# Softplus in a fused FFN–scan–FFN kernel: correction term kept in SBUF, z in two PSUM banks, one ScalarE table set

## The chip, the core and the metric

The kernel runs on one core of a Trainium2 chip. The metric is the device time of one execution in microseconds (us). The engines that matter here are TensorE (PE in the profile, its weight loads PEld), VectorE (DVE), ScalarE (ACT), GpSimd (POOL) and the queue of SyncE (SP), which issues most transfers. Each engine takes its instructions in the order in which they stand in its own program; semaphores tie the engines together.

## The reference

```python
x = x + 0.5 * ffn(layernorm(x), ...)          # x: (4, 512, 256) float32
x = x + attn(layernorm(x), W_x, W_dt, b_dt, A_log, D)
x = x + 0.5 * ffn(layernorm(x), ...)

def attn(x, W_x, W_dt, b_dt, A_log, D):       # a selective scan, 16 states per channel
    x_proj = x @ W_x.T
    dt_x, Bm, Cm = split(x_proj, [R, R + N], axis=-1)       # R = 64, N = 16
    dt = softplus(dt_x @ W_dt.T + b_dt)
    A = -exp(A_log)
    dA = exp(einsum('bld,dn->bldn', dt, A))
    dBx = einsum('bld,bln,bld->bldn', dt, Bm, x)
    h = dA_t * h + dBx_t ; y_t = einsum('bdn,bn->bd', h, C_t)   # for t in order
    return ys + x * D
```

The ffn is a shared expert (gate, up, down) and eight routed experts, of which each token takes one. The change touches only dt = softplus(...) of the middle step and what hangs on it.

## The kernel before, in words

The work has three stages: the first ffn, the scan, the second ffn. In the scan the 4 sequences (batches b) of 512 positions are done one after the other, and in each batch the 16 states n one after the other: state number s = 16 b + n runs from 0 to 63. Channels lie on the 128 partitions in KC = 2 halves k, positions along the free dimension, so a state is a tile of 128 x 1024.

For one state:
- ScalarE computes the decay, `da = exp(a_neg * dt)` (decay, L663, two instructions), three states ahead of the recurrence.
- The input term is `dtx_t * B` with positions on partitions. VectorE and ScalarE share it by quarters (outer, L1405 on VectorE, L679 on ScalarE; the table BY_DVE says how many quarters VectorE takes: 0 for most states), and TensorE transposes it into PSUM (turn_dbx, L1030). For six states of a batch (table DIAG) TensorE forms it itself as a product with a diagonal matrix (L1037), and there is no outer.
- VectorE runs the recurrence over 1024 elements, `hs` (L1421), reading `da` in SBUF and the input term in PSUM.
- GpSimd multiplies it by the row of C, `gs = hs * c_sb` (L523). Both inputs are in SBUF. It runs at most two states ahead of TensorE's add.
- TensorE adds the products, transposed, into the PSUM banks YA (add, L1054), in order; when the 16 states of a batch are added, VectorE adds YA to `x_sb` (add_y, L1457).

While batch b is scanned, the engines prepare dt, B and C of batch b + 1, with these steps put at fixed states n of the loops: project (L983, one matrix product with W_x) into bank T, project_copy on ScalarE (L630) to `proj`, project_bt (L994, TensorE transposes B into bank Y; L1361, VectorE copies it to `b_t`, a part of the tile `h_sb`), project_z (L1003, z = dt_x W_dt^T, one half k at a time, both halves through the one bank T), and then softplus. With w = exp(-|z + b|), softplus is max(z + b, 0) + log(1 + w), and a correction w - ((1 + w) - 1) puts back what the rounding of 1 + w loses. Before: ScalarE takes |z + b| (L636) and max(z + b, 0) (L637) out of the bank, w (L641), 1 + w back into the bank (L650, for b > 0) and the logarithm (L657); VectorE forms the correction in the bank (L1370; for batch 0 it forms 1 + w too, L1373 and L1375), adds the logarithm in the bank (L1381) and then the maximum (L1384), one half at a time. The exponential and the logarithm are in different table sets as loaded here, so each logarithm in the loop has a table load ahead of it (L657) and one behind it (L663). TensorE then transposes dt (turn_dt, L1014) and VectorE multiplies it with xn into `dtx_t` (L1390).

GpSimd also normalises rows for the next stages (L469, SBUF to SBUF): eight instructions ahead of batch 0, then four in each of the batches 0 to 2.

Of the kernel before, what the change touches and what calls it, by code (L numbers as in the profile page):

```python
# [27 lines left out]
def macaron_kernel(nc, x, w_xT, w_dtT, b_dt, a_log, d_skip, router_w, gate_w, up_w, down_w,  # L28
# [47 lines left out]
    with ExitStack() as ctx:  # L76
# [26 lines left out]
        neg_half = sb("neg_half", [P, LT])  # L103
        e_less = sb("e_less", [P, E])
# [123 lines left out]
        pj_all, pj_copy, pj_bt, pj_btc, pj_z, pj_abs, pj_max, pj_exp, pj_u, pj_w, pj_rest, pj_ln, pj_sum, pj_dt, pj_tp, pj_dtx = (  # L228
            sem(f"pj_{s}") for s in ("all", "copy", "bt", "btc", "z", "abs", "max", "exp", "u", "w", "rest", "ln", "sum", "dt", "tp",
# [191 lines left out]
        def _(pool):  # L421
# [135 lines left out]
        def _(act):  # L557
# [85 lines left out]
            def project_u(b, k):  # L643

                if k == 0:
                    act.wait_ge(pj_exp, b + 1)
                    act.wait_ge(pj_max, KC * (b + 1))
                else:
                    act.wait_ge(pj_dt, KC * b + 1)
                nc.scalar.activation(pj_bank(b, k), w_exp[:, k], ACT.Identity, bias=1.0).then_inc(pj_u, 1)  # L650

            def project_ln(b):

                act.wait_ge(pj_exp, b + 1)
                if b > 0:
                    act.wait_ge(pj_sum, KC * b)
# [894 lines left out]
```

## Time and profile before

| what | value |
|---|---|
| median of 3 runs | 441.34 us (440.18 to 441.75) |
| the profiled execution | 441.44 us, of which the span from first to last instruction is 439.6 us |
| busy shares of the span | PE 92%, VectorE 75%, GpSimd 64%, ScalarE 63% |
| mean granted TensorE clock | 0.996 of full speed |
| first ffn, until the scan's first recurrence | 0 to 142.8 us |
| scan, 64 states | 142.8 to about 333 us |
| second ffn | about 333 to 439.6 us |

The shares are means over three stages with different limits. In the scan VectorE, GpSimd, ScalarE and TensorE are all busy most of the time, so there the order in which one releases the other has to be read from the timeline.

### The profile page before, as it was taken

The page shows a single profiled execution, that of the slowest core. Times are in us where ns is not written, and L with a number is a line of the kernel's source. Part 1 is how long each engine was busy: PE and PEld are TensorE (multiplying, and loading weights), DVE is VectorE, ACT ScalarE, POOL GpSimd, SP SyncE. Part 2 cuts the span into 40 slices and gives each one's busy share as a digit, 9 for nine tenths or more (in the row PEclk, how much of TensorE's full clock was granted, in tenths as well). Part 3 has the DMA queues.
Part 4 walks back from the last instruction along what each step waited for, and adds up shares of the span by engine and source line. Part 5 has one row for each costly group of instructions (what it writes and reads, how often), then busy time and mean ns, then how long its engine had stood idle before and what let it go on. Part 6 is the DMA issues. An engine that isn't in the chain of part 4 may idle for free. (4 is left out here: it accounts for less than half of the span.)

```text
span 439.6 us, 8329 instructions
## 1 busy us (share of the span) xinstructions
PE 402.4 (92%) x2716; PEld 278.4 (63%) x2716; DVE 329.5 (75%) x518; ACT 275.0 (63%) x501; POOL 281.1 (64%) x216
## 2 busy tenths in 40 slices
PE   6899899999996899899989997989999899899995
PEld 5537444444454689777977797879994556344452
DVE  4678565553388988999999999989887775456552
ACT  1430465564248799897999899997962210556553
POOL 7204356643328589997999799988891006487553
PEclk9899999999999999999999999999999999999999
DMA  8958115842604226463536453443320534334311
GB/s 250 385 179 264 48 54 167 284 174 101 204 10 91 73 82 180 81 144 106 186 75 118 141 176 73 115 157 92 121 72 0 172 107 120 99 118 135 111 60 48
DMA packets 50808, 56.84 MB, mean 129 GB/s; under 512 B 16329, under 2 KB 35597, under 8 KB 50768
## 3 DMA queue, kind: packets, MB, share of 16 engines
q1 hardware_dynamic: 46624, 45.78, 35.0%
q0 software_dynamic: 4144, 10.54, 8.0%
q8 instruction: 23, 0.38, 0.4%
q14 instruction: 17, 0.14, 0.1%
HBM read 41.14 MB, written 16.48 MB: 131 GB/s over the span
## 5 line engine op out<-in xcount | busy, mean ns | idle before, releaser
L523 POOL TENSOR_TENSOR gs<-hs,c_sb 128x1024 f32<-128x1024 f32 x63 | 148.3, 2380 | 18.7 <-DVE hs L1421 11.4
L1421 DVE TENSOR_TENSOR_SCAN hs<-da,bank 128x1024 f32<-128x1024 f32 x64 | 144.1, 2273 | 4.1 <-PE bank L1030 2.1
L663 ACT ACTIVATE da<-dt_sb,a_neg 128x511 f32<-128x511 f32 x128 | 84.5, 713 | 2.4 <-DVE dt_sb L1384 1.2
L1054 PE MATMUL bank<-ident,gs 128*128 128x128 f32 x504 | 66.3, 275 | 7.5 <-POOL gs L523 5.9
L1054 PEld LDWEIGHTS bank<-ident,gs 128*128 128x128 f32 x504 | 55.9, 141 | 12.1 <-POOL gs L523 9.8
L679 ACT ACTIVATE dbx_t<-dtx_t,h_sb 128x256 f32<-128x256 f32 x145 | 62.1, 498 | 1.6 <-DVE dtx_t L1390 1.4
L879 PE MATMUL bank<-xnT,w_gu 128*128 128x512 f32 x112 | 50.8, 601 | 0.0
L1030 PE MATMUL bank<-ident,dbx_t 128*128 128x128 f32 x336 | 44.2, 274 | 6.8 <-DVE hs L1421 4.1
L477 POOL DMA_INDIRECT da<-rows,row_token x29 | 30.6, 1055 | 29.7 <-DVE row_token L1292 21.2
L1030 PEld LDWEIGHTS bank<-ident,dbx_t 128*128 128x128 f32 x336 | 37.5, 141 | 12.2 <-DVE hs L1421 5.9
L591 ACT ACTIVATE th<-bank,da 128x256 f32<-128x256 f32 x36 | 17.0, 473 | 43.1 <-PE bank L918 30.4
L918 PE MATMUL bank<-w_gu,tt 128*128 x72 | 35.6, 616 | 3.2 <-ACT tt L596 2.2
L498 POOL DMA_INDIRECT token_out<-y_sb,row_token x18 | 19.0, 1056 | 29.2 <-DVE y_sb L1338 26.3
L477 POOL DMA_INDIRECT da<-rows,row_half x14 | 14.7, 1054 | 35.5 <-DVE row_token L1297 27.2
L1328 DVE TENSOR_TENSOR h_sb<-th,bank 128x256 f32<-128x256 f32 x36 | 15.1, 420 | 28.0 <-ACT th L591 27.9
L915 PE MATMUL bank<-w_gu,tt 128*32 x72 | 34.3, 598 | 1.4 <-ACT tt L596 1.4
L879 PEld LDWEIGHTS bank<-xnT,w_gu 128*128 128x128 f32 x112 | 21.0, 194 | 22.4 <-issue 22.3
L915 PE MATMUL bank<-dtx_t,tt 128*32 128x512 f32 x72 | 34.3, 598 | 0.0
L574 ACT ACTIVATE hs<-bank 128x512 f32<-128x512 f32 x10 | 6.0, 597 | 40.0 <-PE bank L879 34.6
L596 ACT ACTIVATE tt<-bank 128x512 f32<-128x512 f32 (+1 forms) x40 | 22.1, 553 | 13.6 <-PE bank L933 12.3
L498 POOL DMA_INDIRECT out<-y_sb,row_token x18 | 19.8, 1098 | 16.1 <-DVE y_sb L1341 8.2
L562 ACT ACTIVATE xnT<-bank 128x512 f32<-128x512 f32 x24 | 13.9, 590 | 17.3 <-PE bank L807 17.2
(184 smaller groups left out, 787.1 us busy)
## 6 DMA issues: line engine op xcount, KB each, us to landing
c_sb<-c_dram SPq DMA_DIRECT2D x64, 256.0 KB, 3.3
rows<-xn_no SPq DMA_DIRECT2D x8, 516.0 KB, 5.4
diag_dram<-dbx_t SPq DMA_DIRECT2D x6, 512.0 KB
routing<-diag_dram SPq DMA_DIRECT2D x11, 256.0 KB, 2.8
slot_m<-diag_dram SPq DMA_DIRECT2D x11, 256.0 KB, 2.9
rows<-xn_no SPq DMA_DIRECT2D x1, 2064.0 KB, 9.4
x_sb<-in_x SPq DMA_DIRECT2D x4, 512.0 KB, 6.4
w_gu<-in_gate_w SPq DMA_DIRECT2D x2, 1024.0 KB, 10.2
```

Of the source, the lines that this page charges most:

```text
L477: nc.gpsimd.indirect_dma_start(out=xr[:, u, lo:hi], out_offset=None, in_=source, in_offset=bass.IndirectOffsetOnAxis(ap=row, axis=0), boun ...
L498: nc.gpsimd.indirect_dma_start(out=rows_back, out_offset=bass.IndirectOffsetOnAxis(ap=row_token[:, TILE[j]:TILE[j] + 1], axis=0), in_=y_sb ...
L523: nc.gpsimd.tensor_tensor(gs[:, s % 2], hs[:, s % RING], c_sb[:, s % RING].unsqueeze(1).to_broadcast([P, KC, L]), ALU.mult).then_inc(sc_g, 1)
L596: nc.scalar.activation(tt[:, (j + 1) % 2, lo:hi], T[:, lo * P:hi * P].rearrange("p (a t) -> p a t", t=P), ACT.Copy).then_inc(ff_tpc, 1)
L663: nc.scalar.activation(da[:, s % RING, k, 1:L], dt_sb[:, k, seq(s // N)][:, 1:L], ACT.Exp, scale=a_neg[:, k, s % N:s % N + 1]).then_inc(sc ...
L679: step = nc.scalar.activation(plain_buffer(s)[:, i, :], dtx_t[:, b % 2, i, :], ACT.Copy, scale=b_t[:, b, i, n:n + 1])
L879: last = nc.tensor.matmul(shared_banks(r, b, fo)[h], w_gu[:, k, SHARED, h * F + fo * P:h * F + (fo + 1) * P], xnT[:, k, b * L:(b + 1) * L] ...
L915: last = nc.tensor.matmul(H[j % 2][part, :], tt[:, j % 2, 2 + k, part], gu_part(i, g)[:, k, :] if g else w, start=(k == 0), stop=(k == KC ...
L918: last = nc.tensor.matmul(H[j % 2][:, :], tt[:, j % 2, 2 + k], w, start=(k == 0), stop=(k == KC - 1))
L1030: mm = nc.tensor.transpose(DBX[s % 2][:, k, i * P:(i + 1) * P], plain_buffer(s)[:, i, k * P:(k + 1) * P], ident[:])
L1054: mm = nc.tensor.matmul(YA[k][:, i * P:(i + 1) * P], products[:, k, i * P:(i + 1) * P], ident[:], start=(s % N == 0 and i == 0), stop=(s % ...
L1421: nc.vector.tensor_tensor_scan(hs[:, s % RING].rearrange(flat), da[:, s % RING].rearrange(flat), DBX[s % 2][:, :, :].rearrange(flat), 0.0, ...
```

## The change

- For batches 1 to 3 z is kept in two banks, T for k = 0 and Y for k = 1 (`pj_bank`). Bank Y held the transposed B, from which VectorE's outer read; outer now reads the copy `b_t` in SBUF.
- B is transposed and copied earlier, since z needs bank Y: on TensorE project_bt stands ahead of turn_dbx at n = 2, 1, 0 of the batches 0, 1, 2 (before: at n = 3), on VectorE the copy stands at n = 3, 2, 1 (before: 4).
- ScalarE no longer takes max(z + b, 0). It writes -(1 + w) once for both halves, 128 x 1024, into an SBUF tile (`neg_u`: half of `dtx_t` for batch 0, `y_sb` later).
- VectorE forms the correction there, (-(1 + w) + 1) + w, in one instruction of 1024 with both inputs in SBUF (project_rest), then max(z + b, correction) per half with z in PSUM (project_max), then adds the logarithm in one instruction of 1024 with both inputs in SBUF (project_dt). dtx is one instruction of 1024 for b > 0.
- One table set that holds exponential and logarithm is loaded ahead of batch 0 and again after the hyperbolic tangent of the shared expert. In the last batch the hyperbolic tangent of the second ffn's first piece has a table load of its own (before: none there).

```diff
         def pj_bank(b, k):
-            return YA[k] if b == 0 else T
+            return (YA if b == 0 else (T, Y))[k]
+
+        def neg_u(b):
+            return dtx_t[:, 1].rearrange("p (k a) d -> p k (a d)", k=KC) if b == 0 else sg_h
...
             def project_abs(b, k):
                 act.wait_ge(pj_z, KC * b + k + 1)
                 if b > 0:
-                    act.wait_ge(pj_rest, KC * b)
+                    act.wait_ge(pj_rest, b)
                 nc.scalar.activation(w_exp[:, k], pj_bank(b, k), ACT.Abs, bias=b_sb[:, k:k + 1]).then_inc(pj_abs, 1)
-                nc.scalar.activation(dt_sb[:, k, seq(b)], pj_bank(b, k), ACT.Relu, bias=b_sb[:, k:k + 1]).then_inc(pj_max, 1)
...
-            def project_u(b, k):
-                if k == 0:
-                    act.wait_ge(pj_exp, b + 1)
-                    act.wait_ge(pj_max, KC * (b + 1))
-                else:
-                    act.wait_ge(pj_dt, KC * b + 1)
-                nc.scalar.activation(pj_bank(b, k), w_exp[:, k], ACT.Identity, bias=1.0).then_inc(pj_u, 1)
+            def project_u(b):
+                act.wait_ge(pj_exp, b + 1)
...
+                nc.scalar.activation(neg_u(b), w_exp[:], ACT.Identity, bias=neg_one[:, 0:1], scale=-1.0).then_inc(pj_u, 1)
...
             def project_bt(b):
                 pe.wait_ge(pj_copy, b + 1)
...
-                    pe.wait_ge(sc_dve, states_by("dve", N * (b - 1) + 4 + 3))
+                    pe.wait_ge(pj_btc, b)
...
             def project_z(b, k):
                 pe.wait_ge(pj_copy, b + 1)
                 if b > 0 and k > 0:
-                    pe.wait_ge(pj_max, KC * b + k)
+                    pe.wait_ge(pj_btc, b + 1)
...
-                    if more and n == 3:
+                    late = (2, 1, 0, 0)[b]
+                    if more and n == late:
                         project_bt(b + 1)
                     if s + 2 < STATES:
                         turn_dbx(s + 2)
...
-                nc.vector.tensor_tensor(pj_bank(b, k), log_w[:, k], pj_bank(b, k),
-                                        ALU.add if b == 0 else ALU.subtract).then_inc(pj_sum, 1)
-                dve.wait_ge(pj_sum, KC * b + k + 1)
-                nc.vector.tensor_tensor(dt_sb[:, k, seq(b)], pj_bank(b, k), dt_sb[:, k, seq(b)], ALU.add).then_inc(pj_dt, 1)
+            def project_rest(b):
+                dve.wait_ge(pj_u, b + 1)
+                nc.vector.scalar_tensor_tensor(out=neg_u(b), in0=neg_u(b), scalar=1.0, in1=w_exp[:],
+                                               op0=ALU.add, op1=ALU.add).then_inc(pj_rest, 1)
+
+            def project_max(b):
+                dve.wait_ge(pj_rest, b + 1)
+                for k in range(KC):
+                    nc.vector.scalar_tensor_tensor(out=neg_u(b)[:, k], in0=pj_bank(b, k), scalar=b_sb[:, k:k + 1], in1=neg_u(b)[:, k],
+                                                   op0=ALU.add, op1=ALU.max).then_inc(pj_max, 1)
+
+            def project_dt(b):
+                dve.wait_ge(pj_ln, b + 1)
+                dve.wait_ge(pj_max, KC * (b + 1))
+                nc.vector.tensor_tensor(dt_sb[:, :, seq(b)], log_w, neg_u(b), ALU.add).then_inc(pj_dt, 1)
...
                 nc.vector.tensor_tensor(plain_buffer(s)[:, LT - mine:, :], dtx_t[:, b % 2, LT - mine:, :],
-                                        B_T[:, b, LT - mine:, n:n + 1].to_broadcast([P, mine, D]), ALU.mult).then_inc(sc_dve, 1)
+                                        b_t[:, b, LT - mine:, n:n + 1].to_broadcast([P, mine, D]), ALU.mult).then_inc(sc_dve, 1)
```

Three places show how instructions move. In these lists the lines of the changed kernel differ by some 5 to 10 from those of the kernel before, the recurrence (L1421, now L1425) is named SCALAR_TENSOR_TENSOR, and x2 means two alike in a row.

TensorE at the seam from batch 1 to batch 2, before: the product with W_x (L983), the transposes of the input term (L1030) and the adds (L1054).

```order
L983 MATMUL bank<-xnT,w_x 96x512 x2
L1030 MATMUL bank<-ident,dbx_t 128x128 x8
L1054 MATMUL bank<-ident,gs 128x128 x8
L1003 MATMUL bank<-th,w_dt 128x512
L1030 MATMUL bank<-ident,dbx_t 128x128 x8
```

The same place in the changed kernel:

```order
L990 MATMUL bank<-xnT,w_x 96x512 x2
L1001 MATMUL bank<-ident,th 128x16 x4
L1035 MATMUL bank<-ident,dbx_t 128x128 x8
L1059 MATMUL bank<-ident,gs 128x128 x8
L1010 MATMUL bank<-th,w_dt 128x512
L1035 MATMUL bank<-ident,dbx_t 128x128 x8
```

The four transposes of B out of `proj` (the tile `th`) now stand right behind the product with W_x, ahead of the last add of batch 1. The same move is made in batch 0, where they stand ahead of turn_dbx(4).

VectorE in the middle of batch 1 (the recurrences of states 21 to 24 and what stands between), before:

```order
L1421 SCALAR_TENSOR_TENSOR hs<-da,bank 128x1024
L1370 SCALAR_TENSOR_TENSOR bank<-bank,w_exp 128x512
L1421 SCALAR_TENSOR_TENSOR hs<-da,bank 128x1024
L1381 TENSOR_TENSOR bank<-tt,bank 128x512
L1384 TENSOR_TENSOR dt_sb<-bank,dt_sb 128x512
L1421 SCALAR_TENSOR_TENSOR hs<-da,bank 128x1024
L1370 SCALAR_TENSOR_TENSOR bank<-bank,w_exp 128x512
L1405 TENSOR_TENSOR dbx_t<-dtx_t,bank 128x256
L1421 SCALAR_TENSOR_TENSOR hs<-da,bank 128x1024
```

In the changed kernel, from the recurrences of states 19 to 21 on:

```order
L1425 SCALAR_TENSOR_TENSOR hs<-da,bank 128x1024 x3
L1371 SCALAR_TENSOR_TENSOR y_sb<-y_sb,w_exp 128x1024
L1425 SCALAR_TENSOR_TENSOR hs<-da,bank 128x1024
L1378 SCALAR_TENSOR_TENSOR y_sb<-bank,b_sb,y_sb 128x512 x2
L1425 SCALAR_TENSOR_TENSOR hs<-da,bank 128x1024
L1385 TENSOR_TENSOR dt_sb<-tt,y_sb 128x2x512
L1409 TENSOR_TENSOR dbx_t<-dtx_t,h_sb 128x256
L1425 SCALAR_TENSOR_TENSOR hs<-da,bank 128x1024 x2
```

Every one of the steps before had one input in a PSUM bank; now L1371, L1385 and L1409 take both from SBUF tiles.

VectorE ahead of the first recurrence, before, from the correction to the first outer:

```order
L1373 TENSOR_SCALAR bank<-w_exp 128x512
L1375 TENSOR_TENSOR bank<-w_exp,bank 128x512
L1373 TENSOR_SCALAR bank<-w_exp 128x512
L1375 TENSOR_TENSOR bank<-w_exp,bank 128x512
L1381 TENSOR_TENSOR bank<-tt,bank 128x512
L1384 TENSOR_TENSOR dt_sb<-bank,dt_sb 128x512
L1381 TENSOR_TENSOR bank<-tt,bank 128x512
L1384 TENSOR_TENSOR dt_sb<-bank,dt_sb 128x512
L1390 TENSOR_TENSOR dtx_t<-bank,xn_no 128x512 x2
L1405 TENSOR_TENSOR dbx_t<-dtx_t,bank 128x512
```

The same stretch in the changed kernel:

```order
L1371 SCALAR_TENSOR_TENSOR dtx_t<-dtx_t,w_exp 128x1024
L1378 SCALAR_TENSOR_TENSOR dtx_t<-bank,b_sb,dtx_t 128x512 x2
L1385 TENSOR_TENSOR dt_sb<-tt,dtx_t 128x2x512
L1393 TENSOR_TENSOR dtx_t<-bank,xn_no 128x512 x2
L1409 TENSOR_TENSOR dbx_t<-dtx_t,h_sb 128x512
```

Eight instructions of 512 have become two of 512 and two of 1024.

## Rows read from the trace of the kernel before

**Rows 1.** Busy us by engine (PE, PEld, DVE, ACT, POOL), batch by batch

```profile
156.00:197.60 41.60, 38.85 (x315) 34.58 (x315) 38.62 (x37) 39.02 (x71) 40.67 (x21) 1.00 0.51 126
197.60:244.20 46.60, 43.99 (x353) 38.64 (x352) 45.11 (x42) 44.00 (x82) 43.81 (x23) 1.00 0.49 127
244.20:291.00 46.80, 43.27 (x353) 39.22 (x354) 45.52 (x41) 44.06 (x82) 43.93 (x23) 1.00 0.42 126
291.00:333.50 42.50, 40.66 (x321) 37.44 (x320) 38.58 (x34) 31.02 (x65) 34.06 (x18) 1.00 0.32 94
```

**Rows 2.** Timeline, GpSimd in batch 1: start, us, idle before in brackets

```profile
205.02 2.36 POOL L523 TENSOR_TENSOR gs<-hs,c_sb 128x1024 f32<-128x1024 f32 x1 [1.51 <-DVE hs L1421]
...
225.29 18.72 POOL L523 TENSOR_TENSOR gs<-hs,c_sb 128x1024 f32<-128x1024 f32 x8
```

**Rows 3.** Groups by line: busy us, mean ns, idle before and releaser

```profile
L523 POOL TENSOR_TENSOR gs<-hs,c_sb 128x1024 f32<-128x1024 f32 x63 | 148.3, 2380 | 18.7 <-DVE hs L1421 11.4 <-PE bank L1054 7.1
L1421 DVE TENSOR_TENSOR_SCAN hs<-da,bank 128x1024 f32<-128x1024 f32 x64 | 144.1, 2273 | 4.1 <-PE bank L1030 2.1 <-PE bank L1037 2.0
...
L637 ACT ACTIVATE dt_sb<-bank,b_sb 128x512 f32<-128x512 f32 x8 | 5.5, 682 | 0.0
...
L657 ACT ACT_TABLE_LOAD x4 | 5.1, 1283 | 0.1
...
L1357 DVE TENSOR_TENSOR x_sb<-xn_no,x_sb 128x1024 f32<-128x1024 f32 x3 | 3.7, 1222 | 2.7 <-DMA xn_no<-token_out 2.7
...
L1405 DVE TENSOR_TENSOR dbx_t<-dtx_t,bank 128x256 f32<-128x256 f32 x17 | 6.8, 402 | 0.1
...
L1381 DVE TENSOR_TENSOR bank<-tt,bank 128x512 f32<-128x512 f32 x8 | 5.5, 682 | 1.0 <-ACT tt L657 1.0
L1390 DVE TENSOR_TENSOR dtx_t<-bank,xn_no 128x512 f32<-128x512 f32 x8 | 5.3, 671 | 0.8 <-PE bank L1014 0.8
...
L1370 DVE SCALAR_TENSOR_TENSOR bank<-bank,w_exp 128x512 f32<-128x512 f32 x6 | 4.1, 678 | 0.7 <-ACT bank L650 0.7
```

**Rows 4.** Line L1450 (min/median/max ns), and the timeline around it

```profile
L1450 DVE TENSOR_TENSOR dbx_t<-hs,c_sb x2: 678/968/1259, 329.4 to 330.6; 128x512 f32<-128x512 f32 x2
...
327.78 2.35 POOL L523 TENSOR_TENSOR gs<-hs,c_sb 128x1024 f32<-128x1024 f32 x1 [0.52 <-PE bank L1054]
...
329.42 1.86 DVE L1450 TENSOR_TENSOR dbx_t<-hs,c_sb 128x512 f32<-128x512 f32 x2
```

**Rows 5.** Timeline ahead of the first recurrence, GpSimd and VectorE

```profile
131.37 9.65 POOL L469 TENSOR_SCALAR xn_no<-x_sb,mv,rstd 128x256 f32<-128x256 f32 x8
...
132.12 0.69 DVE L1373 TENSOR_SCALAR bank<-w_exp 128x512 f32<-128x512 f32 x1 [1.37 <-ACT w_exp L641]
...
136.83 0.69 DVE L1384 TENSOR_TENSOR dt_sb<-bank,dt_sb 128x512 f32<-128x512 f32 x1
...
142.78 2.28 DVE L1421 TENSOR_TENSOR_SCAN hs<-da,bank 128x1024 f32<-128x1024 f32 x1
```

**Rows 6.** Timeline of the first states of batch 0

```profile
145.15 4.87 POOL L523 TENSOR_TENSOR gs<-hs,c_sb 128x1024 f32<-128x1024 f32 x2 [4.12 <-DVE hs L1421]
...
148.07 0.41 DVE L1405 TENSOR_TENSOR dbx_t<-dtx_t,bank 128x256 f32<-128x256 f32 x1
...
153.96 1.04 PE L1030 MATMUL bank<-ident,dbx_t 128*128 128x128 f32 x8
...
154.16 0.59 ACT L630 ACTIVATE th<-bank 96x512 f32<-96x512 f32 x1 [2.26 <-PE bank L983]
```

**Rows 7.** Timeline at the seam from batch 1 to batch 2

```profile
240.52 1.88 PE L983 MATMUL bank<-xnT,w_x 128*96 128x512 f32 x4
...
242.68 0.58 ACT L630 ACTIVATE th<-bank 96x512 f32<-96x512 f32 x1
...
243.11 1.04 PE L1054 MATMUL bank<-ident,gs 128*128 128x128 f32 x8
...
244.19 1.28 DVE L1457 TENSOR_TENSOR x_sb<-x_sb,bank 128x512 f32<-128x512 f32 x2 [0.83 <-PE bank L1054]
```

More of the change, by code:

```diff
@@ L103, in macaron_kernel @@
         neg_half = sb("neg_half", [P, LT])
+        neg_one = sb("neg_one", [P, 1])
         e_less = sb("e_less", [P, E])
@@ L227, in macaron_kernel @@
         a_ready = sem("a_ready")
-        pj_all, pj_copy, pj_bt, pj_btc, pj_z, pj_abs, pj_max, pj_exp, pj_u, pj_w, pj_rest, pj_ln, pj_sum, pj_dt, pj_tp, pj_dtx = (
-            sem(f"pj_{s}") for s in ("all", "copy", "bt", "btc", "z", "abs", "max", "exp", "u", "w", "rest", "ln", "sum", "dt", "tp",
+        pj_all, pj_copy, pj_bt, pj_btc, pj_z, pj_abs, pj_max, pj_exp, pj_u, pj_rest, pj_ln, pj_dt, pj_tp, pj_dtx = (
+            sem(f"pj_{s}") for s in ("all", "copy", "bt", "btc", "z", "abs", "max", "exp", "u", "rest", "ln", "dt", "tp",
                                      "dtx"))
@@ L701, in scan @@
                         project_exp(1)
-                        project_u(1, 0)
-                    if b < BATCH - 1 and n == 7 + int(b == 0):
-                        project_u(b + 1, 1)
+                    if b == 0 and n == 5:
+                        project_u(1)
                     if b == 0 and n == 6:
@@ L1005, in turn_dt @@
             def turn_dt(b, h):
-                pe.wait_ge(pj_dt, KC * (b + 1))
-                if b > 0 and h > 0:
-                    pe.wait_ge(pj_dtx, 2 * b + h)
-                dst = YA[h] if b == 0 else T
+                pe.wait_ge(pj_dt, b + 1)
+                dst = pj_bank(b, h)
                 for i in range(2):
@@ L1089, in scan @@
                         skip(b, n - 5)
-                    if more and n - int(b == 0) in (8, 10):
-                        turn_dt(b + 1, (n - 8) // 2)
+                    if more and n - int(b == 0) in (8, 9):
+                        turn_dt(b + 1, n - int(b == 0) - 8)
                     turn = 12 if more else 9
@@ new lines, in project_dtx @@
+            def project_dtx(b):
+                halves = ((0, 1), (1, 2)) if b == 0 else ((0, 2),)
+                for lo, hi in halves:
+                    dve.wait_ge(pj_tp, 2 * b + hi)
+                    src = pair[3 if b == 0 else 1][:, lo:hi].rearrange("p h (i d) -> p (h i) d", d=D)
+                    nc.vector.tensor_tensor(dtx_t[:, b % 2, 2 * lo:2 * hi], src, xn[:, LT * b + 2 * lo:LT * b + 2 * hi, :],
+                                            ALU.mult).then_inc(pj_dtx, hi - lo)
@@ L1434, in scan @@
                         stats_of(2, b - 1)
-                    if more and n == 4:
+                    late = int(b == 0)
+                    if more and n == (3, 2, 1)[b]:
                         project_bt(b + 1)
-                    late = int(b == 0)
-                    if more and n in (5 + late, 7 + late):
-                        project_w(b + 1, (n - 5) // 2)
-                    if more and n in (6 + late, 8 + late):
-                        project_dt(b + 1, (n - 6) // 2)
-                    if more and n in (10 + late, 12 + late):
-                        project_dtx(b + 1, (n - 10) // 2)
+                    if more and n == 5 + late:
+                        project_rest(b + 1)
+                    if more and n == 6 + late:
+                        project_max(b + 1)
+                    if more and n == 7 + late:
+                        project_dt(b + 1)
+                    if more and n == 11 + late:
+                        project_dtx(b + 1)
             def last_product():
@@ L1492, in _ @@
             shared_hidden(0, 3, 0)
-            for k in range(KC):
-                project_w(0, k)
-            for k in range(KC):
-                project_dt(0, k)
-            for h in range(2):
-                project_dtx(0, h)
+            project_rest(0)
+            project_max(0)
+            project_dt(0)
+            project_dtx(0)
             outer(0)
```

42 lines of the change are left out of this document (15 added, 27 removed).

## The prediction

> **What bounds the kernel now.** I read the busy time of each engine batch by batch first. In a batch of the scan VectorE works 45 of 46.6 us, TensorE 44, ScalarE 44, GpSimd 44 [rows 1], so a share alone names no bound; the waits must. The timeline of GpSimd shows them: in batch 1, once its product of state 19 has started at 205.02, it runs without a gap through its other steps to the eight products that end at 244.0 [rows 2]; in batches 0 and 2 it does the same from the sixth and fifth state on. A product takes 2.38 us, a recurrence on VectorE 2.27 [rows 3] (2.2 from start to start), so VectorE makes its states a little faster and spends the rest on softplus and outer. For most of each batch GpSimd paces the adds and VectorE has little to spare. At a seam the order is fixed: TensorE's last add, then VectorE's add_y, which waited 0.83 us for it [rows 7], then the next recurrences. The ffn stages ahead of and behind the scan hold nothing of the change.
>
> **What the change takes away.** Per batch ScalarE loses two maxima of 0.68 us and, for batches 1 to 3, two table loads of 1.28 [rows 3], some 3.9 us. Nothing on the path waits for ScalarE but VectorE for 1.0 us before L1381 and 0.7 before L1370 in the whole run [rows 3]. VectorE loses eight steps of 0.67 to 0.69 [rows 3], 5.4 us, and gets three of 1024 at 1.22 (L1357 is the nearest row: two SBUF inputs, 1024) and two of 512 at 0.68, 5.0 us: 0.4 less. In a stretch that GpSimd paces, both savings hide behind GpSimd's products; where VectorE paced instead they would be worth 0.4 x 3 + 1.7 = 2.9 us.
>
> **What it adds: two SBUF inputs beside GpSimd.** No VectorE instruction of the scan before reads two SBUF tiles, but one: L1450. It ran twice, 512 wide, alike in shape: 1.26 us and 0.68 [rows 4]. The first was issued at 329.42, while GpSimd's product ran from 327.78 to 330.13, and ended at 330.68: it did next to nothing until GpSimd had finished and then needed 0.55 us. I take it that the two cannot read together. The page SBUF — State Buffer of the Trainium skill, section "Who interferes with whom", says the same: a VectorE instruction with two SBUF inputs contends with a GpSimd instruction that reads SBUF, the first to start holds the shared pair for its whole length and the other is fully blocked. By that rule the trace agrees (1.26 against 0.68), and it speaks against this change; with the rule the sum is the one below, and read the other way, as no collision, it is the first rival's.
>
> The change gives VectorE such steps in the middle of GpSimd's busy stretches: project_rest and project_dt once per batch, and every outer. If VectorE comes while GpSimd works, it waits for that product's end (0 to 2.38 us); then GpSimd's next one waits until VectorE is done. That second half no row shows. Bounds for what it costs GpSimd: nothing, to VectorE's whole step. I take what was left of the step in rows 4, 0.55 per 512: 1.1 us for 1024, 0.27 for an outer of 256. The steps, in order:
> - Ahead of the first recurrence. Without collisions this gets shorter: one maximum less ahead of w (about 0.57 from start to start), -(1 + w) at about 1.06 more, then 1.22, 1.2 and 1.22 in place of the steps from 132.12 to 137.52 [rows 5]: dt about 1.2 us earlier. But GpSimd normalises from 131.37 to 141.02, eight times 1.21 [rows 5]. Stepped: project_rest, ready at 132.6, has just missed the end at 132.58, runs from 133.8 to 134.9; the maxima to 136.2; project_dt at the next end, 137.3 to 138.4; the first outer to 141.3; the second waits for the last normalisation, pushed to 143.8; first recurrence at 144.95 against 142.78 [rows 5], +2.2. If project_rest slips in ahead of the instruction at 132.58, it comes at 143.85, +1.1. I take 1.7.
> - First states. The outer at 148.07 meets GpSimd's second product, which ends at 150.02 [rows 6]: +1.9 for the recurrence behind it, and for the add, project and all that follow. Then project_bt stands ahead of turn_dbx(4) and needs project_copy, which ended at 154.75 (154.16 + 0.59), where TensorE had started turn_dbx(4) at 153.96 [rows 6]: 0.8 of waiting and about 0.42 of transposes, 1.25. GpSimd had 0.4 us idle soon after, which swallows that much: 1.9 + 1.25 - 0.4 = 2.75.
> - The rest of batch 0, paced by GpSimd: project_rest and project_dt 2.2, outers of the states 10, 12, 16 and 17 at 0.27, 1.1: 3.3.
> - Batch 1: 2.2 and five outers (26, 28, 30, 32, 33), 1.35: 3.55. At its end TensorE's four transposes of B stand ahead of turn_dbx and the last add. They need project_copy, and that needs project, which ran from 240.52 to 242.4; the copy came at 242.68 to 243.26 on a ScalarE that was just free [rows 7]; now it may start 0.1 earlier. TensorE would stand from 242.24 to 243.2 and then transpose for 0.42: the add at 243.11 [rows 7] comes 1.4 later, and VectorE's add_y, already waiting for it, too. Of that 0.2 may be won back, as the add before starts the sooner: 1.2. Together 4.75.
> - Batch 2: 2.2 and three outers (42, 44, 46), 0.8: 3.0. Its seam has no such transposes.
> - Batch 3 has no outer on VectorE. Its one new table load, 1.28 [rows 3], stands on ScalarE with 31.0 of 42.5 us busy [rows 1] and three states ahead: 0.1.
> Sum: 1.7 + 2.75 + 3.3 + 4.75 + 3.0 + 0.1 = 15.6. The profiled execution took 441.44 us, its span 439.6 and 1.84 around it; the median is 441.34. **I predict 457.0 us.** Low end for the mechanism: half of the steps meet GpSimd between two products, about 449. High end: VectorE's waits, on average half a product, are not hidden but pace the batch. Six in batch 0, seven in 1, five in 2, each 1.2, less what VectorE had to spare (3.0, 1.5 and 1.3 us of idle time [rows 1], and the 0.4 saved): 3.8 + 6.5 + 4.3 in place of 3.3 + 3.55 + 3.0, about 462, and 466 with a start at +3.4 and a wait more at a seam.
>
> **Rivals.**
> *No collision worth speaking of.* The 1.26 us of L1450 had another cause (it is one instruction), or a step of 0.4 us finds a gap. Then: start -1.2, first states 1.25 - 0.4, the seam 1.2, the rest hidden by GpSimd's pace: +0.9, 442.3 us. Against it: the end of L1450 falls 0.55 us behind GpSimd's, as waiting would have it.
> *Faster.* No collision, and VectorE, not GpSimd, paces: then its 2.9 us come off and the start's 1.2, and the two stalls of TensorE are swallowed: 437.3 us. For it: VectorE has the highest busy time in batches 1 and 2 [rows 1]. Against it: GpSimd has no gap in the states 19 to 32 [rows 2], and add_y waits for an add that stands behind its product. It decides if VectorE's new steps of 1024 take 1.2 us in the scan and GpSimd's chain has gaps.
> *GpSimd does not let go.* Its instructions follow each other without a gap, so a waiting VectorE step could be passed over until GpSimd runs out of states. One product more, 2.38 less the 1.2 already counted, at each of the some 16 steps: +19, 476 us.
> *The table sets are not merged after all.* The order of the changed kernel has no table load around the logarithms; and ScalarE bounds nothing, so the time would not tell.
>
> **How the numbers follow.** Collision as stepped: 0.70, its own range 449 to 466. No collision: 0.15 (440.5 to 444.5). Faster: 0.08. GpSimd does not let go: 0.07. About 0.5%, 2.2 us, is what a measurement of this kernel can tell from no change. Slower by more: 0.70 + 0.07 + 0.03 of the no-collision case = 0.80; within: 0.11; faster: 0.08 + 0.01 = 0.09. The range reaches from 440.5, which takes in nearly all of the no-collision case, to 468, and leaves out the faster case, the last rival and a little more: 2 in 10.
>
> **What the profile of the changed kernel would show.** Right: L1409 (outer, 256) mean near 1 to 1.5 us in place of 0.40, with some at 0.40 and some over 2; L1371 and L1385 over 1.22, in the loop up to 3; gaps in GpSimd's chain of products right behind them; TensorE idle ahead of L1001 twice, near 0.8 and 1.0 us; the first recurrence at 144 to 145 us and a scan of about 204 us in place of 190; ScalarE some 12 us less busy and waiting. Wrong: L1409 at 0.40 throughout and GpSimd's chain without new gaps (no collision); the same with the first recurrence near 141.6 and shorter batches (faster); a GpSimd chain as before with VectorE steps of 3 to 5 us (the last rival). The sum would also be wrong if VectorE and GpSimd fall into step so that outers always come at a product's end: then only the 2.2 us per batch and the stalls of TensorE are left, near 450.

## The result, and the profile after

The changed kernel takes **456.66 us** (median of 4 runs, 455.58 to 458.0), the kernel before 440.81 beside it (440.18 to 441.75): ratio 1.036, 95% interval 1.032 to 1.040. It is slower by 3.6%, as predicted (457.0). The profiled execution took 456.64 us, its span 454.9, so 15.3 us more of span where the sum said 15.6. Of the four executions of e5 below, the longest, 459.67 us, was in the chip's slower state and is left out of its median and ratio.

The busy time of each engine from the first recurrence on, cut at VectorE's four add_y (columns: stretch, its length, PE, PEld, DVE, ACT, POOL, granted clock, DMA share, GB/s; compare [rows 1]), changed kernel:

```profile
142.58:204.51 61.93, 52.56 (x388) 45.50 (x387) 57.88 (x43) 45.35 (x85) 50.28 (x25) 0.97 0.42 103
204.51:255.03 50.52, 45.20 (x357) 39.09 (x356) 47.06 (x38) 40.86 (x77) 46.73 (x23) 1.00 0.44 115
255.03:302.75 47.72, 42.32 (x341) 37.75 (x342) 45.96 (x35) 38.52 (x73) 44.71 (x22) 1.00 0.40 114
302.75:347.45 44.70, 42.62 (x325) 39.83 (x324) 39.12 (x34) 33.87 (x69) 35.67 (x19) 0.96 0.30 95
```

Every batch is longer, the last too, and in the first and the last the mean clock is below 1. The same cuts in all kernels of this study (us, from the timeline of VectorE in each one's profiled execution; a fall is a stretch in which TensorE's granted clock is 0.50, 1.2 of 2.4 GHz, lasting 3.4 us where nothing else is said):

| kernel | first recurrence at | batch 0 | 1 | 2 | 3 | falls of the clock in it |
|---|---|---|---|---|---|---|
| before | 142.78 | 54.79 | 46.62 | 45.20 | 42.80 | none |
| after | 142.58 | 61.93 | 50.52 | 47.72 | 44.70 | batches 0, 3 |
| e1, before with outers from SBUF | 142.54 | 63.86 | 48.59 | 46.88 | 42.81 | batch 0: 6.8 us and 3.4 |
| e2, after, outers to ScalarE | 143.10 | 56.93 | 52.13 | 47.24 | 43.05 | batch 1 |
| e3, after, B's transposes late | 142.76 | 61.07 | 49.24 | 47.70 | 44.73 | batches 0, 3 |
| e5, after, operands in PSUM | 141.76 | 62.71 | 53.75 | 45.81 | 43.05 | batch 0: 6.8 us and 3.4; batch 1: 6.8 us |
| e10, e2 and e3 | 142.10 | 56.47 | 48.41 | 47.29 | 44.71 | batch 3 |
| e6, e2, e3 and e5 | 144.93 | 54.70 | 46.48 | 45.63 | 43.03 | ahead of the scan: two |
| e8, after, TensorE kept busy twice | 144.35 | 62.14 | 50.47 | 47.75 | 43.52 | ahead of the scan, batch 0 |
| e9, the same, three times | 143.25 | 61.04 | 50.50 | 47.75 | 43.52 | none |

What lies behind the last add_y is 107.4 us in both kernels. Groups by line, changed kernel (busy us, mean ns; outer, project_rest, project_dt of the loop, and GpSimd's normalisations):

```profile
L1409 DVE TENSOR_TENSOR dbx_t<-dtx_t,h_sb 128x256 f32<-128x256 f32 x17 | 13.1, 773 | 0.0
...
L1371 DVE SCALAR_TENSOR_TENSOR y_sb<-y_sb,w_exp 128x1024 f32<-128x1024 f32 x3 | 7.7, 2573 | 0.0
...
L1385 DVE TENSOR_TENSOR dt_sb<-tt,y_sb 128x1024 f32<-128x1024 f32 x3 | 5.0, 1651 | 0.0
...
L476 POOL TENSOR_SCALAR xn_no<-x_sb,mv,rstd 128x256 f32<-128x256 f32 x20 | 29.9, 1500 | 0.0
...
L1371 DVE SCALAR_TENSOR_TENSOR dtx_t<-dtx_t,w_exp 128x1024 f32<-128x1024 f32 x1 | 1.3, 1260 | 1.8 <-ACT dtx_t L658 1.8
```

Outer has a mean of 0.77 us where it had 0.40 [rows 3], and project_rest takes 2.57 in the loop where the one ahead of the loop, which came just as an instruction of GpSimd ended, took 1.26. GpSimd's normalisation, 1.21 each in [rows 5], has a mean of 1.50: it waits too. The timeline of batch 1 shows both directions:

```profile
215.82 5.67 POOL L530 TENSOR_TENSOR gs<-hs,c_sb 128x1024 f32<-128x1024 f32 x2
216.36 2.92 DVE L1371 SCALAR_TENSOR_TENSOR y_sb<-y_sb,w_exp 128x1024 f32<-128x1024 f32 x1
...
224.90 1.22 DVE L1385 TENSOR_TENSOR dt_sb<-tt,y_sb 128x1024 f32<-128x1024 f32 x1
225.02 2.44 POOL L476 TENSOR_SCALAR xn_no<-x_sb,mv,rstd 128x256 f32<-128x256 f32 x1
```

Project_rest is issued 0.54 us into a product, waits for its end and holds up the next: two products take 5.67 us in place of 4.76 (2 x 2.38, [rows 3]). Project_dt comes at 224.90, with 0.13 us left of the product that runs, takes its 1.22 us, and the normalisation behind it takes 2.44 (an outer follows project_dt at once).

The first states of batch 0, changed kernel (compare [rows 6]):

```profile
144.94 4.86 POOL L530 TENSOR_TENSOR gs<-hs,c_sb 128x1024 f32<-128x1024 f32 x2 [2.15 <-DVE hs L1425]
...
147.87 2.21 DVE L1409 TENSOR_TENSOR dbx_t<-dtx_t,h_sb 128x256 f32<-128x256 f32 x1
150.01 2.27 DVE L1425 TENSOR_TENSOR_SCAN hs<-da,bank 128x1024 f32<-128x1024 f32 x1
...
152.92 1.09 PE L1059 MATMUL bank<-ident,gs 128*128 128x128 f32 x8 [3.68 <-DVE x_sb L1308]
...
156.41 0.42 PE L1001 MATMUL bank<-ident,th 16*128 16x16 f32 x4 [0.68 <-ACT th L637]
```

The outer of state 4 took 2.21 us instead of 0.41 because GpSimd's second product had just begun. VectorE's next steps slip, TensorE's first add waits 3.68 us for one of them, and behind project it stands 0.68 us for project_copy. The granted clock in two stretches of 2 us of batch 0 (the column behind the five engines), and the transposes on TensorE at which the falls of batches 0 and 3 began, changed kernel:

```profile
194.00:196.00 2.00, 0.81 (x5) 0.81 (x6) 2.00 (x3) 0.83 (x2) 1.93 (x2) 0.87 0.86 88
196.00:198.00 2.00, 2.00 (x12) 2.00 (x10) 2.00 (x2) 2.00 (x5) 1.68 (x1) 0.50 0.59 165
...
195.19 1.73 PE L1035 MATMUL bank<-ident,dbx_t 128*128 128x128 f32 x8 [1.39 <-DVE hs L1425]
...
311.19 1.68 PE L1035 MATMUL bank<-ident,dbx_t 128*128 128x128 f32 x8 [1.98 <-DVE hs L1425]
```

After a pause TensorE's clock fell to its lower level. The eight transposes took 1.7 us where they take 1.04 [rows 6].

### The profile page after: what moved, and what is told of

The parts are those of the page before. It is cut to its first block and busy times, and to the rows that moved or that the text cites. A ratio compares the mean times of both kernels' runs of the same rounds, so it can differ in the third digit from the quotient of the medians.

```text
span 454.9 us, 8294 instructions
## 1 busy us (share of the span) xinstructions
PE 406.6 (89%) x2716; PEld 280.0 (62%) x2716; DVE 339.8 (75%) x505; ACT 266.2 (59%) x486; POOL 290.4 (64%) x217
## 5 line engine op out<-in xcount | busy, mean ns | idle before, releaser
L530 POOL TENSOR_TENSOR gs<-hs,c_sb 128x1024 f32<-128x1024 f32 x63 | 151.3, 2419 | 24.6 <-PE bank L1059 14.4
L1425 DVE TENSOR_TENSOR_SCAN hs<-da,bank 128x1024 f32<-128x1024 f32 x64 | 143.8, 2271 | 3.8 <-PE bank L1035 1.9
L1059 PE MATMUL bank<-ident,gs 128*128 128x128 f32 x504 | 68.2, 280 | 12.3 <-POOL gs L530 8.1
L1059 PEld LDWEIGHTS bank<-ident,gs 128*128 128x128 f32 x504 | 57.6, 143 | 18.0 <-POOL gs L530 14.0
L1035 PE MATMUL bank<-ident,dbx_t 128*128 128x128 f32 x336 | 45.5, 280 | 7.0 <-DVE hs L1425 4.3
L476 POOL TENSOR_SCALAR xn_no<-x_sb,mv,rstd 128x256 f32<-128x256 f32 x20 | 29.9, 1500 | 0.0
L505 POOL DMA_INDIRECT out<-y_sb,row_token x18 | 18.7, 1037 | 16.8 <-DVE y_sb L1346 9.4
```

What stands on the lines that cost most here:

```text
L476: nc.gpsimd.tensor_scalar(xn[:, i], x_sb[:, i, :], mv[:, i, 0:1], rstd[:, i:i + 1], ALU.subtract, ALU.mult).then_inc(ln_xn, 1)
L505: nc.gpsimd.indirect_dma_start(out=rows_back, out_offset=bass.IndirectOffsetOnAxis(ap=row_token[:, TILE[j]:TILE[j] + 1], axis=0), in_=y_sb ...
L530: nc.gpsimd.tensor_tensor(gs[:, s % 2], hs[:, s % RING], c_sb[:, s % RING].unsqueeze(1).to_broadcast([P, KC, L]), ALU.mult).then_inc(sc_g, 1)
L1035: mm = nc.tensor.transpose(DBX[s % 2][:, k, i * P:(i + 1) * P], plain_buffer(s)[:, i, k * P:(k + 1) * P], ident[:])
L1059: mm = nc.tensor.matmul(YA[k][:, i * P:(i + 1) * P], products[:, k, i * P:(i + 1) * P], ident[:], start=(s % N == 0 and i == 0), stop=(s % ...
L1425: nc.vector.tensor_tensor_scan(hs[:, s % RING].rearrange(flat), da[:, s % RING].rearrange(flat), DBX[s % 2][:, :, :].rearrange(flat), 0.0, ...
```

## The experiments

**The outers alone (e1).** The kernel before, with one operand moved, and a wait for the copy that it now reads:

```diff
                 if n == 0:
                     dve.wait_ge(pj_dtx, 2 * (b + 1))
+                    dve.wait_ge(pj_btc, b + 1)
                 nc.vector.tensor_tensor(plain_buffer(s)[:, LT - mine:, :], dtx_t[:, b % 2, LT - mine:, :],
-                                        B_T[:, b, LT - mine:, n:n + 1].to_broadcast([P, mine, D]), ALU.mult).then_inc(sc_dve, 1)
+                                        b_t[:, b, LT - mine:, n:n + 1].to_broadcast([P, mine, D]), ALU.mult).then_inc(sc_dve, 1)
```

> The kernel before, with one thing of the change in it: the outers of VectorE read B from its copy b_t in SBUF instead of from PSUM. Theory (two SBUF inputs and GpSimd's reads exclude each other): the outer of state 4 takes about 2.2 us instead of 0.40 and delays the recurrence behind it by 1.6 to 1.9; several of the 19 others wait too, or make a product start up to 0.4 us late: 443 to 447 us against 441, mean outer 0.7 to 0.9 us instead of 0.40. Rival (the outers do not collide; only the new steps of 1024 and TensorE's order cost): 441 within 1, every outer at 0.40 us.

453.95 us, ratio 1.026 (1.022 to 1.030). The mechanism is there, but the size is missed by 7 us. The timeline of e1:

```profile
147.84 2.23 DVE L1406 TENSOR_TENSOR dbx_t<-dtx_t,h_sb 128x256 f32<-128x256 f32 x1
...
152.90 1.97 PE L1054 MATMUL bank<-ident,gs 128*128 128x128 f32 x8 [3.42 <-DVE x_sb L1303]
154.65 3.62 PE L983 MATMUL bank<-xnT,w_x 128*96 128x512 f32 x4
...
185.80 4.68 POOL L523 TENSOR_TENSOR gs<-hs,c_sb 128x1024 f32<-128x1024 f32 x2
186.17 4.59 DVE L1406 TENSOR_TENSOR dbx_t<-dtx_t,h_sb 128x256 f32<-128x256 f32 x1
```

Two things were not in the sum. Toward the end of the pause of 3.42 us the clock fell, for 6.8 us, so that the add and project took about twice their time; it fell once more, for 3.4 us, later in batch 0. And at 186.17 an outer was passed over once at a product's end: two products ran without a gap and it took 4.59 us. That is the rival "GpSimd does not let go", once in 20 outers. Where neither happened, in batches 1 and 2, the outers cost 2.0 and 1.7 us.

**The outers taken away (e2).** The changed kernel with

```diff
-    BY_DVE = ((2, 2, 2, 1, 1, 1) + (0,) * 6 + (1, 0, 1, 0),) + ((1, 1, 0, 1) + (0,) * 6 + (1, 0, 1, 0, 1, 0),) * 2 + ((0,) * 16,)
+    BY_DVE = ((2, 2, 2, 1) + (0,) * 12,) + ((0,) * 16,) * 3
```

> The changed kernel with all outers from state 4 on given to ScalarE, which does such a quarter in 0.43 us and has 6 to 9 us of idle time per batch. Project_rest and project_dt, with their two SBUF inputs, stay. Theory: the outer of state 4 no longer holds the fifth recurrence (1.6 to 1.9 us), the blocked outer at 191.15 in batch 0 is gone and with it the idle time of TensorE after which its clock fell (about 2 us), and the others give back some 1 to 2 us: 450 to 453 us against 456.7. Rival (the outers cost nothing, the steps of 1024 are the whole loss): 456 to 457. Second rival: ScalarE becomes late with its outers and the time rises over 457.

451.11 us, ratio 1.019 (1.014 to 1.025): as the theory had it. Batch 0 is 5.0 us shorter and its fall is gone; another came at the seam, in batch 1.

**TensorE's order (e3).**

```diff
-                    if more and n == late:
-                        project_bt(b + 1)
                     if s + 2 < STATES:
                         turn_dbx(s + 2)
...
+                    if more and n == late:
+                        project_bt(b + 1)
                     if more and n in (late, late + 1):
                         project_z(b + 1, n - late)
```

> The changed kernel with the four transposes of B put back behind turn_dbx and the add of the same state, just ahead of project_z. Theory: TensorE no longer stands 0.7 us for project_copy ahead of L1001 in batch 0 and 0.7 us at the end of batch 1, and the transposes' 0.42 us leave the way to the last add: 1.25 less in the first states, 1.2 less at the seam, together 2 to 2.5 us: 454.2 to 454.7. Rival (what TensorE waits is hidden behind GpSimd's products): 456.7 within 0.7.

454.13 us, ratio 1.027 (1.022 to 1.032), just below the theory's range by the median (a little more gained than it said), though the interval meets that of the changed kernel. The trace is plainer: batch 1 is 1.28 us shorter, with no fall in it in either kernel.

**The softplus with one SBUF input per step (e5).**

```diff
+                nc.scalar.activation(pj_bank(b, k), pj_bank(b, k), ACT.Relu, bias=b_sb[:, k:k + 1]).then_inc(pj_max, 1)
...
-                nc.vector.scalar_tensor_tensor(out=neg_u(b), in0=neg_u(b), scalar=1.0, in1=w_exp[:],
+                nc.vector.scalar_tensor_tensor(out=project_both(b), in0=neg_u(b), scalar=1.0, in1=project_both(b),
...
-                for k in range(KC):
-                    nc.vector.scalar_tensor_tensor(out=neg_u(b)[:, k], in0=pj_bank(b, k), scalar=b_sb[:, k:k + 1], in1=neg_u(b)[:, k],
-                                                   op0=ALU.add, op1=ALU.max).then_inc(pj_max, 1)
+                nc.vector.tensor_tensor(project_both(b), w_exp[:], project_both(b), ALU.add).then_inc(pj_rest, 1)
...
-                nc.vector.tensor_tensor(dt_sb[:, :, seq(b)], log_w, neg_u(b), ALU.add).then_inc(pj_dt, 1)
+                nc.vector.tensor_tensor(dt_sb[:, :, seq(b)], log_w, project_both(b), ALU.add).then_inc(pj_dt, 1)
```

The tile project_both is z's two PSUM banks read and written as one.

> The changed kernel with a softplus that has one SBUF input at most per VectorE step: ScalarE writes max(z + b, 0) over z in the two PSUM banks (two steps of 0.68 us per batch, as in the kernel before), VectorE adds 1 and -(1 + w) to it there, then w, then log(1 + w): three steps of 1024, each with one SBUF and one PSUM input. The outers still read two SBUF tiles. Theory: the three steps take about 1.22 us each wherever they fall, GpSimd is not held by them, and the 2.2 us per batch that project_rest and project_dt cost on GpSimd's chain go: 5 to 6 us less over batches 0 to 2, 450 to 452 us. Rival (only outers and TensorE's order cost): 456 to 458, since VectorE works 1.2 us per batch less two maxima of 0.7 more or less the same.

454.16 us (452.67 to 456.24, three runs), ratio 1.025 (1.019 to 1.031): between the theory's range and the rival's, by itself inconclusive. Batch 2, without a fall, is 1.9 us shorter, but in the profiled execution the clock fell for 17.1 us in all in batches 0 and 1, which hides the rest.

**Only the two steps of 1024 left (e10).** The edits of e2 and e3 together.

> The changed kernel with the outers from state 4 on at ScalarE and B's transposes back behind the add, but with project_rest and project_dt as the change has them. Against the kernel with all three undone (443.1) it holds the price of these two steps of 1024 with two SBUF inputs. Theory: some 2 us a batch in batches 0 to 2, 448 to 450 us. Rival (these two steps fall on time that VectorE has to spare, and the outers were all that mattered): 443 to 445.

448.17 us, ratio 1.015 (1.013 to 1.018). The theory's range holds. Batches 0 to 2, free of falls, are 1.7, 1.8 and 2.1 us longer than before, and 1.8, 1.9 and 1.7 longer than in e6 below, from which e10 differs by the edit of e5 alone. Per batch, project_rest and project_dt together take about that much more than 1.22 us each (groups by line of e10):

```profile
L1371 DVE SCALAR_TENSOR_TENSOR y_sb<-y_sb,w_exp 128x1024 f32<-128x1024 f32 x3 | 7.9, 2642 | 0.0
L1385 DVE TENSOR_TENSOR dt_sb<-tt,y_sb 128x1024 f32<-128x1024 f32 x3 | 5.0, 1655 | 0.0
```

**All three undone (e6).** The edits of e2, e3 and e5.

> The three edits before in one: outers from state 4 on given to ScalarE, the softplus with at most one SBUF input per VectorE step, B's transposes back behind the add. What stays of the change is z in two banks, one table set, and VectorE's steps of 1024. Theory (collisions, TensorE's order and the clock are the whole loss): no VectorE step of the softplus above 1.3 us, no fall of the clock, 440 to 443 us against 441.5. Rival (something else of the change costs too, such as ScalarE's added work, now 43 to 44 us a batch): 445 to 449.

443.12 us, ratio 1.003 (1.001 to 1.004): what was lost is back but for some 1 to 2 us. Its new steps, in the groups by line of e6, take 1.20 to 1.22 us in the mean, so GpSimd does not hold them:

```profile
L1383 DVE TENSOR_TENSOR bank<-w_exp,bank 128x1024 f32<-128x1024 f32 x4 | 4.8, 1212 | 0.0
L1389 DVE TENSOR_TENSOR dt_sb<-tt,bank 128x1024 f32<-128x1024 f32 x4 | 4.8, 1201 | 0.1
L1377 DVE SCALAR_TENSOR_TENSOR bank<-y_sb,bank 128x1024 f32<-128x1024 f32 x3 | 3.7, 1221 | 0.9 <-ACT y_sb L660 0.9
```

The median lies just above the theory's end. Its profiled execution was one of the longest (443.94); its batches are those of before within 0.5 us and its first recurrence came 2.15 us later, behind falls ahead of the scan. That the other runs lost their time there too is not shown.

**TensorE kept busy in the pauses (e8, e9).** The changed kernel with matrix products of a constant tile with itself (`warm`):

```diff
+                    if s + 2 in (16, 53):                       # e8, e9
+                        pe.wait_ge(pj_dtx, 2 * BATCH if s + 2 == 53 else 4)
+                        warm(Y, 12 if s + 2 == 53 else 8)
                     if s + 2 < STATES:
                         turn_dbx(s + 2)
...
+                    if s == 1:                                  # e9 alone
+                        warm(Y, 20)
                     if s > 0:
                         add(s - 1)
```

> The changed kernel with TensorE kept at work in the two pauses after which its granted clock fell (193.80 to 195.19 in batch 0, 309.22 to 311.19 in batch 3): 8 transposes of a constant tile (0.13 us each) ahead of the turn_dbx at 195.19 and 12 ahead of that at 311.19, into a PSUM bank that nobody reads then; nothing else is changed. Theory (the clock, not GpSimd, made batch 3 longer by 1.9 us, and took some 1.9 of the 4.1 that the rest of batch 0 lost): no fall of the clock at these two places, batch 3 from add_y to add_y back at 42.8 to 43.0 us instead of 44.7, batch 0 about 1.5 to 2 us shorter, 453 us in all unless the clock falls elsewhere. Rival (the slow clock is hidden behind GpSimd): 456.7 within 0.7, and batch 3 still at 44.7.

> The changed kernel with TensorE kept at work in three pauses: the two before, and the 3.7 us ahead of the first add (20 transposes of a constant tile there), behind which the clock fell at 155.5 in the kernel with two. Theory (falls of the clock behind pauses cost 1.7 us each): no fall in the scan, 452.5 to 454 us. Rival (they come elsewhere, or are worth little): 455.5 to 457.

e8: 455.47 us, ratio 1.031 (1.028 to 1.035), between the theory's 453 and the rival's range. Neither fall came where it had been, and batch 3 took 43.52 us instead of 44.70, against 43.03 to 43.05 in e2, e5 and e6, which pause there without a fall. The 12 products make the difference: they took longer than the 0.13 us each of the expectation,

```profile
311.01 2.84 PE L793 MATMUL bank<-ident 128*128 128x128 f32 x24
```

so that turn_dbx came 2.5 us behind the add instead of 2.0. But the clock fell at two other places. e9: 454.90 us, ratio 1.030 (1.028 to 1.033), 1.8 us less than the change by the medians (the intervals of the two ratios just meet), above the theory's range and below the rival's. Its profiled execution has no fall in the scan and takes 202.8 us from the first recurrence to the last add_y, the changed kernel 204.9: 0.9 less in batch 0, 1.2 in batch 3, nothing in between. In batch 0 the way to the fifth recurrence, with the 20 products in it, is 0.6 us longer and the rest 1.5 shorter. So a fall cost some 1.5 to 1.7 us, as the theory had it, and the products took about 1 us of that back. The clock is not the main cause of the loss: without a fall in the scan, e9 still takes 3.0% more than the kernel before.

**One table set alone (e4), and relief for GpSimd (f3, f6, f4).** e4 is the kernel before with the two loads of the change. f3 adds to it

```diff
-                    if 0 < b < BATCH - 1 and 5 <= n < 5 + LT:      # GpSimd
-                        normalise(2, b - 1, (n - 5,))
...
-                    if not more and 6 <= n < 6 + LT:               # ScalarE
+                    if b > 0 and 6 <= n < 6 + LT:
                         normalise(b - 1, n - 6)
```

f6 is f3 with the outers from state 12 on at ScalarE, f4 is e6 with f3's edit.

> The kernel before with the one table set for Exp and Ln and nothing else. ScalarE loses its table loads around the logarithms, 2.6 us a batch. Theory (ScalarE is off the path, VectorE waited 1.7 us for it in the whole run): 440.5 to 441.5 us, the same within 0.3%. Rival (ScalarE's loads delay softplus and with it VectorE): 437 to 439 us.

> The kernel before with the one table set, and with the four normalisations per batch of batches 1 and 2 moved from GpSimd (1.22 us each) to ScalarE (0.43 us each), which the table loads had filled. GpSimd loses about 4.2 us net in each of these two batches. Theory (GpSimd paces the batches, VectorE is right behind it with 45.1 of 46.6 us): each of the two batches gets 0.8 to 1.4 us shorter, until VectorE paces: 438.5 to 440 us. Rival (the adds at the seam or ScalarE set the pace): 441 to 442.

> The kernel before with the one table set, the normalisations of batches 1 and 2 on ScalarE instead of GpSimd, and the outers from state 12 of each batch on as well on ScalarE instead of VectorE. GpSimd has 39.8 us of work in batch 1 then, VectorE 43.8, ScalarE 44.4, TensorE 43.6. Theory (relieving GpSimd alone gave next to nothing because VectorE was as full; both have to be relieved): batches 1 and 2 each 0.8 to 1.3 us shorter than before, 439 to 440 us. Rival (TensorE and the order of the states set the pace, or ScalarE becomes late): 441 to 443.

> The kernel with all three undone, and the normalisations of batches 1 and 2 on ScalarE instead of GpSimd. VectorE has 42.9 us of work in batch 1, GpSimd 39.8, TensorE 43.9, ScalarE about 45. Theory (with VectorE relieved, GpSimd paced that kernel): batches 1 and 2 each 0.8 to 1.5 us shorter than in it, 440 to 441.5 us. Rival (ScalarE, now the fullest, is late): 443 to 445.

e4: 441.94 us, ratio 1.002 (1.000 to 1.004), no change, as the theory said. f3: 442.07, ratio 1.001 (0.999 to 1.003). f6: 444.47, 1.007 (1.005 to 1.009), with falls of the clock where the scan begins (6.8 us) and in batch 3. f4: 443.0, 1.004 (1.002 to 1.007). All three missed: none is faster than before. The windows of batch 1 and batch 2, f3:

```profile
198.58:244.76 46.18, 43.58 (x353) 38.69 (x352) 45.02 (x42) 42.82 (x84) 39.80 (x21) 1.00 0.52 133
244.76:290.09 45.33, 41.43 (x345) 37.93 (x346) 43.93 (x39) 41.83 (x82) 39.37 (x20) 1.00 0.43 126
```

GpSimd has 4.0 us less to do in batch 1 than in [rows 1], and the batch gets 0.4 us shorter, batch 2 no shorter; in f4, where VectorE has 2.2 us less as well, batch 1 takes 46.54. But in f4 ScalarE, which took the work over, is busy for 44.1 us of these 46.54, so its own lateness, the rival on record, is not excluded there. No version of this study beats the kernel before.

## Why the prediction held, step by step

| step of the sum | predicted | measured (profiled executions) |
|---|---|---|
| ahead of the first recurrence | +1.7 | -0.2 |
| first states (to the fifth recurrence) | +2.75 | +3.06 |
| rest of batch 0 | +3.3 | +4.08 |
| batch 1 and its seam | +4.75 | +3.90 |
| batch 2 | +3.0 | +2.52 |
| batch 3 | +0.1 | +1.90 |
| sum | +15.6 | +15.3 |

Of the signs that the prediction named, the scan (204.9 us, 204 said), the long project_rest and project_dt and the gaps behind them came. L1409's mean is 0.77 us where 1 to 1.5 was said, TensorE stood 0.68 us ahead of L1001 both times (0.8 and 1.0 said), ScalarE is 8.8 us less busy (some 12 said, with its waits), and the first recurrence came at 142.58, not 144 to 145.

**The mechanism** is shown from both sides. A VectorE step with two SBUF inputs and GpSimd's products hold each other up: adding such inputs to the outers of the kernel before costs 2.6%, some of it clock (e1), taking them all away, with TensorE's order, gives the loss back (e6). The rule of the Trainium skill (SBUF — State Buffer, section "Who interferes with whom"), that the first to start holds the shared pair for its whole length and the other is blocked, agrees for the products with both directions in the rows of batch 1 above (5.67 us for two products, 2.92 for project_rest). For GpSimd's normalisations it does not agree, as the paragraph on the start shows, and there the measurement decides.

**By cause.** Project_rest and project_dt: predicted 2.2 us in each of three batches, 6.6; measured 5.6 (e10 against before) or 5.4 (e10 against e6). The outers: predicted 1.9 + 1.1 + 1.35 + 0.8 = 5.15; from e3 to e10 the ratio falls from 1.027 to 1.015, some 5 us, some of it clock. In batch 1 they cost 0.8, in batch 2 0.4 (e3 against e10, no falls), less than 1.35 and 0.8, and batch 0 pays most: of the 6.3 us that 17 outers take longer (13.1 against 6.8 [rows 3]), 5.7 lie in four outers there, 2.21, 1.79, 1.69 and 1.57 us long. In the other batches most come near the end of a product or of a normalisation, much as the prediction named it as a way to be wrong. TensorE's order at the seam: predicted 1.2, measured 1.28 (e3). TensorE's order in the first states: predicted 1.25 - 0.4, measured some 0.5 (batch 0 of e2 against e10). The outer of state 4: predicted 1.9; without it and that of state 5, e2 takes 13.17 us from the first to the fifth recurrence, the changed kernel 15.31, so 2.1.

**The start was mis-sized.** The prediction let each VectorE step with two SBUF inputs wait for the end of the normalisation that it meets, and so bounded the start at +1.1 to +2.2; a gain of 1.2 was kept for the rival without collisions. No such wait came. The timeline of the changed kernel (compare [rows 5]), with two of GpSimd's eight normalisations by themselves as well:

```profile
131.11 11.68 POOL L476 TENSOR_SCALAR xn_no<-x_sb,mv,rstd 128x256 f32<-128x256 f32 x8
...
132.31 1.26 DVE L1371 SCALAR_TENSOR_TENSOR dtx_t<-dtx_t,w_exp 128x1024 f32<-128x1024 f32 x1 [1.82 <-ACT dtx_t L658]
...
134.58 1.21 POOL L476 TENSOR_SCALAR xn_no<-x_sb,mv,rstd 128x256 f32<-128x256 f32 x1
135.12 1.23 DVE L1385 TENSOR_TENSOR dt_sb<-tt,dtx_t 128x1024 f32<-128x1024 f32 x1
...
137.78 1.29 DVE L1393 TENSOR_TENSOR dtx_t<-bank,xn_no 128x512 f32<-128x512 f32 x2 [1.43 <-PE bank L1019]
...
138.63 1.22 POOL L476 TENSOR_SCALAR xn_no<-x_sb,mv,rstd 128x256 f32<-128x256 f32 x1
139.16 0.69 DVE L1409 TENSOR_TENSOR dbx_t<-dtx_t,h_sb 128x512 f32<-128x512 f32 x1
```

Project_rest came just before a normalisation's end, and the next one waited for it. Project_dt began 0.54 us into a normalisation, with 0.67 us of it left, and the first outer 0.53 us into another, with 0.69 left. Both took their own length, 1.23 and 0.69 us, and so did these two normalisations. So a normalisation does not hold VectorE off for the whole of its recorded length, as a product does (the outer at 147.87). Which part of it does is not measured: one outer ahead of the scan took 0.97 us instead of 0.68 beside a normalisation. The eight normalisations took 11.68 us instead of 9.65, where nobody waits for GpSimd, and dt was ready 1.2 us earlier. Of that only 0.2 reached the first recurrence: VectorE waited 1.43 us for TensorE's transposes of dt (0.8 in [rows 3]), and two outers took 1.57 us instead of 1.28. The step had no bound for a collision that costs VectorE nothing.

**Batch 3 was missed for another reason.** Of its 1.9 us, 1.65 are a fall of the clock (44.70 to 44.73 us with one, 43.03 to 43.05 without). The rest, 0.25, is the table load, foreseen at 0.1: with nothing but the one table set, e4, the last batch takes 43.07 us against 42.80. In the rest of batch 0 a fall is in the measured 4.08 as well, some 1.5 us (e9 without it), so that the collisions there cost about 2.6 and not 3.3. No term of the sum was for the clock. Its some 3.1 us made up for the terms that were too large: the start by 1.9, batch 1 by 0.85, the rest of batch 0 by 0.7, batch 2 by 0.5. The right total is in part luck, two errors that cancel.

**That GpSimd paces the batches** is not borne out. Without 4 us of its work f3 is no faster. The terms of the collisions came out near anyway, since each collision holds both engines: e10's project_rest and project_dt wait 1.4 and 0.4 us beyond their own length in the mean, 1.8 a batch, which is about what a batch lost. Batch by batch they wait 2.3, 1.5 and 1.7 us, and GpSimd loses some 1.9 in each, where the batches lost 1.7, 1.8 and 2.1: GpSimd's loss is the nearer one, but that does not decide it. Which of the two the batch pays, and what sets its 46 us when either engine is relieved, stays open.

## What to carry to other kernels

Before an operand is moved from PSUM to SBUF, count the SBUF inputs that the VectorE instruction has then, and look what GpSimd does at that place: a step of 0.40 us became 2.2 here. Such a step holds up both engines, itself in its own wait and GpSimd in its next instruction, and it costs once more where TensorE pauses behind it and its clock falls. It matters what GpSimd does there: beside its products the steps waited, in a normalisation two of them did not. Making an engine's work smaller bought nothing here where it was not shown first that the engine's wait ends last: fewer table loads on ScalarE (e4) and fewer normalisations on GpSimd (f3) gave no time at all.

## What the runs showed of the hardware that I had not expected

- TensorE's granted clock fell to 0.50 (1.2 of 2.4 GHz) in the scan of eight of the fourteen profiled executions, for 3.4 or 6.8 us, in the changed kernel behind pauses of 1.4 and 2.0 us. A pause alone does not decide it: the 3.68 us ahead of the first add of the changed kernel were followed by full clock, the 3.67 us at the same place in e3 by a fall; in e1 the clock fell 1.1 us before the 3.42 us there were over. And e2, e5 and e6 paused 2.0 us in batch 3, ahead of the same transposes as the changed kernel at 311.19, without a fall. What decides is open.
- A VectorE step that waits for a product of GpSimd usually starts at the product's end, though GpSimd's next instruction is ready; once, in e1, it was passed over and waited 4.2 us. The two steps that came 0.5 us into a normalisation of 1.2 us (ahead of the scan of the changed kernel) did not wait.
